# Gate shares by tanh in the graph stage, a root in the last norm, and VectorE sums for the interleaved groups

## What is computed

```python
n   = layernorm(x)                                  # no scale, no offset
agg = epsilon * n + adj @ n                         # per graph, 128x128
h   = silu(rmsnorm(agg @ W1 + b1, rms_weight))      # 512 wide
x   = x + h @ W2 + b2

u   = layernorm(x)
top_v, top_i = top_k(u @ gate_w + gate_b, 2)        # of 16 experts
w   = softmax(top_v)                                # two shares per node
expert(e, u) = relu(u @ w1[e] + b1[e]) @ w2[e] + b2[e]      # 256 wide
moe = w[0] * expert(top_i[0], u) + w[1] * expert(top_i[1], u)
x   = x + layernorm(u + moe) * gamma + beta
```

## Time and profile before

| | |
|---|---|
| median of 3 runs | 896.23 us (894.04 to 896.98) |
| the profiled execution | 895.33 us, span 893.5 us |
| mean granted TensorE clock | 0.955 |
| PE busy | 798.2 us, 89% |
| DVE busy | 644.9 us, 72% |
| ACT busy | 619.6 us, 69% |
| POOL busy | 541.7 us, 61% |
| DMA | 145.20 MB, mean 163 GB/s |

### The profile page before, as it was taken

The page is one execution under the profiler, slowest core; times in us unless marked ns, Lnnn a source line. Parts: engine busy times, 40 slices in busy tenths (PEclk is TensorE's granted clock), DMA queues, the critical chain, the costliest instruction groups (busy, mean ns, idle before and its releaser), DMA issues. The chain is left out here.

```text
span 893.5 us, 20763 instructions
## 1 busy us (share of the span) xinstructions
PE 798.2 (89%) x4835; PEld 593.5 (66%) x4836; DVE 644.9 (72%) x2646; ACT 619.6 (69%) x1327; POOL 541.7 (61%) x572
## 2 busy tenths in 40 slices
PE   5899999999999999943999999999999999999662
PEld 4577777777777777742777777666666666666320
DVE  3688989989999998865566665666766667666444
ACT  2699999999999999841443333666666666666787
POOL 2007766776676767676677777766666656666400
PEclk9799999999999999975999999999999999999875
DMA  5323444333343322217666668877788777777251
GB/s 152 95 72 119 122 121 119 119 119 119 116 119 119 107 83 73 79 54 219 193 200 196 196 210 257 262 223 224 226 241 240 232 232 222 232 223 225 85 193 65
DMA packets 104172, 145.20 MB, mean 163 GB/s; under 512 B 17537, under 2 KB 56855, under 8 KB 104119
## 3 DMA queue, kind: packets, MB, share of 16 engines
q1 hardware_dynamic: 84582, 109.16, 42.8%
q0 software_dynamic: 17344, 34.13, 10.7%
q10 hardware_dynamic: 2192, 1.31, 0.5%
HBM read 99.67 MB, written 46.81 MB: 164 GB/s over the span
## 5 line engine op out<-in xcount | busy, mean ns | idle before, releaser
L467 POOL DMA_INDIRECT combined<-tout,tdest x286 | 282.7, 988 | 131.6 <-issue 73.5
L454 POOL DMA_INDIRECT dispatched<-rows,slot_i x256 | 253.3, 989 | 167.1 <-DVE slot_i L1008 89.8
L782 ACT ACTIVATE hid<-bank,wts 128x256 f32<-128x256 f32 x286 | 119.4, 470 | 169.1 <-PE bank L647 167.5
L662 PE MATMUL bank<-wts,hid 128*128 128x128 f32 x1144 | 165.6, 288 | 0.0
L1117 DVE SCALAR_TENSOR_TENSOR tout<-bank,gate,tin 128x128 f32<-128x128 f32 x286 | 87.1, 346 | 92.5 <-PE bank L662 89.5
L662 PEld LDWEIGHTS bank<-wts,hid 128*128 128x128 f32 x1144 | 138.4, 191 | 17.1
L647 PE MATMUL bank<-tut,wts 128*128 128x256 f32 x572 | 148.6, 383 | 0.0
L502 PEld LDWEIGHTS bank<-w_sb,work 128*128 128x128 f32 x1024 | 122.9, 193 | 17.7 <-issue 14.6
L502 PE MATMUL bank<-w_sb,work 128*128 128x128 f32 x1024 | 126.1, 277 | 1.9 <-ACT work L763 1.9
L496 PE MATMUL bank<-agg,w_sb 128*128 128x512 f32 x256 | 125.0, 611 | 0.0
L647 PEld LDWEIGHTS bank<-tut,wts 128*128 128x128 f32 x572 | 98.6, 193 | 7.6
(11 more groups left out here) (158 smaller groups left out, 1229.1 us busy)
## 6 DMA issues: line engine op xcount, KB each, us to landing
wts<-in_w_exp SPq DMA_DIRECT2D x143, 257.0 KB
tin<-dispatched SPq DMA_DIRECT2D x143, 132.0 KB
moe<-combined SPq DMA_DIRECT2D x32, 512.0 KB
xs<-in_x SPq DMA_DIRECT2D x32, 256.0 KB, 3.0
adj_sb<-in_adj_t SPq DMA_DIRECT2D x32, 256.0 KB
rms_b<-r_row SPq DMA_DIRECT2D x32, 256.0 KB, 3.5
out<-agg SPq DMA_DIRECT2D x32, 256.0 KB, 5.0
combined<-tout,tdest POOLq DMA_INDIRECT x286
```

Of the source, the lines that this page charges most:

```text
L454: nc.gpsimd.indirect_dma_start(dispatched, bass.IndirectOffsetOnAxis(slot_i[:, k, n:n + 1], 0), rows[:, k, n // TOPK, n % TOPK, :], None). ...
L467: nc.gpsimd.indirect_dma_start(combined, bass.IndirectOffsetOnAxis(tdest[:, k, a:a + 1], 0), tout[:, k, a, :], None, bounds_check=TOK * TO ...
L662: last = nc.tensor.matmul(exp_ps[n % 2][:, a * D:(a + 1) * D], hid[:, n % 2, c, a * P:(a + 1) * P], wts[:, k, F + c * D:F + (c + 1) * D], ...
L782: last = nc.scalar.activation(hid[:, n % 2, c, :], hid_ps[n % 2][:, c * TILE:(c + 1) * TILE], ACT.Relu, bias=wts[:, k, F + FC * D + c:F + ...
```

## The change

- DVE writes the difference of the two gate values with its sign to the row (two instructions of 128x4 in place of one of 128x8), and ACT replaces it in the graph stage by tanh(difference / 2), after the first of the four Silus. POOL waits for this (`tanh_done`) in place of `gap_done`. In the tile stage the share is then 0.5 x tanh + 0.5, one DVE instruction; the Exp on ACT and the sum, reciprocal and product on DVE are gone.
- The scale of the last norm is Sqrt on ACT and a reciprocal on DVE, in the next post step, in place of Ln and Exp on ACT.
- For groups 0 to 23 DVE adds the two expert results in SBUF, in place, and takes the statistics there; ACT normalizes from SBUF. PE does no sum for them. The `moe` buffer now holds the sum until ACT has read it, so SP waits for `p_n` in place of `p_y` before it loads a group of the first 24 + 3. Groups 24 to 31 are summed by PE as before.
- One more block of `mixed` is unrolled in front of the loop, which has one turn less.

```diff
+        def summed_by_dve(i, g):
+            return i is not None or g < MIXED
+        def y_of(i, g, k):
+            return moe[:, k, :, 0, :] if summed_by_dve(i, g) else y_ps[k].rearrange("p (j d) -> p j d", d=D)
...
@@ sp, post_step @@
-                    if g >= RING:
-                        sp.wait_ge(p_y, count(i, g - RING + 1))
+                    if i is None and g - RING >= MIXED:
+                        sp.wait_ge(p_y, g - RING - MIXED + 1)
+                    elif g >= RING:
+                        sp.wait_ge(p_n, count(i, g - RING + 1))
...
@@ pool, step @@
-                    pool.wait_ge(gap_done, count(i, g + 1))
+                    pool.wait_ge(tanh_done, count(i, g + 1))
...
@@ pe, post_step @@
-                if has(i, g):
+                if i is None and MIXED <= g < NG:
                     k = g % RING
                     pe.wait_ge(moe_in[k], count(i, g // RING + 1, 16, 1))
-                    if g >= RING:
-                        pe.wait_ge(p_n, count(i, g - RING + 1))
+                    if g - RING >= MIXED:
+                        pe.wait_ge(p_n, g - RING + 1)
...
@@ act, step @@
+                def half_gap(g):
+                    act.wait_ge(gap_done, count(i, g + 1))
+                    gap = rows[:, g % RING, :, :, D + 1:D + 2].rearrange("p j c o -> p (j c o)")
+                    nc.scalar.activation(gap, gap, ACT.Tanh, scale=0.5).then_inc(tanh_done, 1)
+                if not has(i, t) and has(i, t - 3):
+                    half_gap(t - 3)
...
                         nc.scalar.activation(z, z, ACT.Silu, scale=rms_sb[:, c:c + 1]).then_inc(s_done, 1)
+                        if c == 0 and has(i, t - 3):
+                            half_gap(t - 3)
...
@@ act, tile_step @@
-                    if n >= 2:
-                        act.wait_ge(t_gate, count(i, n - 1, 1, RING2 * m))
-                    nc.scalar.activation(share[:, n % 2], tin[:, k, :, D + 1:D + 1 + TOPK], ACT.Exp)\
-                        .then_inc(t_exp, 1)
...
@@ act, post_step @@
-                    nc.scalar.activation(sd[:, 0, k, :], bn[:, 0, k, :, 2], ACT.Ln, bias=ln_eps[:, 0:1],
-                                         scale=1.0 / D).then_inc(p_sd, 1)
-                    act.wait_ge(p_sd, count(i, g + 1))
-                    nc.scalar.activation(rs[:, 0, k, :], sd[:, 0, k, :], ACT.Exp, scale=-0.5).then_inc(p_rs, 1)
+                    nc.scalar.activation(sd[:, 0, k, :], bn[:, 0, k, :, 2], ACT.Sqrt, bias=ln_eps[:, 0:1],
+                                         scale=1.0 / D)\
+                        .then_inc(p_sd, 1)
...
@@ dve, tile_step @@
-                    nc.vector.tensor_tensor(share_sum[:, n % 2], share[:, n % 2, :, 0], share[:, n % 2, :, 1],
-                                            ALU.add).then_inc(t_sum, 1)
-                    dve.wait_ge(t_sum, count(i, n + 1, 1, RING2 * m))
-                    nc.vector.reciprocal(share_inv[:, n % 2], share_sum[:, n % 2]).then_inc(t_inv, 1)
+                    nc.vector.tensor_scalar(gate[:, n % 2], tin[:, k, :, D + 1], 0.5, 0.5, ALU.mult, ALU.add)\
+                        .then_inc(t_gate, 1)
...
@@ dve, post_step, ahead of nb @@
+                    dve.wait_ge(p_sd, count(i, g + 1))
+                    nc.vector.reciprocal(rs[:, 0, k], sd[:, 0, k, :]).then_inc(p_rs, 1)
...
-                    dve.wait_ge(p_y, count(i, g + 1))
+                    if summed_by_dve(i, g):
+                        dve.wait_ge(moe_in[k], count(i, g // RING + 1, 16, 1))
+                        nc.vector.tensor_tensor(moe[:, k, :, 0, :], moe[:, k, :, 0, :], moe[:, k, :, 1, :],
+                                                ALU.add).then_inc(p_sum, 1)
+                        dve.wait_ge(p_sum, count(i, g + 1))
+                    else:
+                        dve.wait_ge(p_y, g - MIXED + 1)
```

More of the change, by code:

```diff
@@ L29 @@
 MIX_FROM = 43
-MIX_TURNS = 5
-MIXED = RING * (3 + MIX_TURNS)
+MIX_TURNS = 4
+MIXED = RING * (4 + MIX_TURNS)
 NQ = NS * E
@@ L151, in gnn_moe @@
         tdest = sb("tdest", [P, RING2, TH], i32)
-        share = sb("share", [P, 2, TH, TOPK])
-        share_sum = sb("share_sum", [P, 2, TH])
-        share_inv = sb("share_inv", [P, 2, TH])
         gate = sb("gate", [P, 2, TH])
@@ L216, in gnn_moe @@
         gap_done = sem("gap_done")
+        tanh_done = sem("tanh_done")
         rank_done = sem("rank_done")
@@ L243, in gnn_moe @@
         t_relu = sem("t_relu")
-        t_exp = sem("t_exp")
-        t_sum = sem("t_sum")
-        t_inv = sem("t_inv")
         t_gate = sem("t_gate")
@@ L253, in gnn_moe @@
         p_y = sem("p_y")
+        p_sum = sem("p_sum")
         p_bn = sem("p_bn")
@@ L294, in tiles_and_groups @@
             span = RING * GB
-            mixed(None, MIX_FROM, -2)
-            mixed(None, MIX_FROM + span, RING - 2)
+            for b in range(3):
+                mixed(None, MIX_FROM + b * span, b * RING - 2)
             with eng.Fori(0, MIX_TURNS) as i:
-                mixed(i, MIX_FROM + 2 * span, 2 * RING - 2)
-            mixed(None, MIX_FROM + (2 + MIX_TURNS) * span, (2 + MIX_TURNS) * RING - 2)
-            for t in range(MIX_FROM + (3 + MIX_TURNS) * span, NT + 1):
+                mixed(i, MIX_FROM + 3 * span, 3 * RING - 2)
+            mixed(None, MIX_FROM + (3 + MIX_TURNS) * span, (3 + MIX_TURNS) * RING - 2)
+            for t in range(MIX_FROM + (4 + MIX_TURNS) * span, NT + 1):
                 tile_step(None, t)
@@ L799, in post_step @@
                     for j in range(GB):
-                        last = nc.scalar.activation(n3[:, k, j, :], y_ps[k][:, j * D:(j + 1) * D], ACT.Identity,
+                        last = nc.scalar.activation(n3[:, k, j, :], y_of(i, g, k)[:, j, :], ACT.Identity,
                                                     bias=nb[:, 0, k, j:j + 1], scale=rs[:, 0, k, j:j + 1])
@@ L956, in step @@
                     last.then_inc(topi_done, 1)
[L957 to L960, removed]
+                    nc.vector.tensor_tensor(rows[:, k, :, 0, D + 1:D + 2], top_v[:, :, 0:1], top_v[:, :, 1:2],
+                                            ALU.subtract)
+                    nc.vector.tensor_tensor(rows[:, k, :, 1, D + 1:D + 2], top_v[:, :, 1:2], top_v[:, :, 0:1],
+                                            ALU.subtract).then_inc(gap_done, 1)
                     dve.wait_ge(topi_done, count(i, g + 1))
@@ L1096, in tile_step @@
                     k = n % RING2
-                    dve.wait_ge(t_exp, count(i, n + 1, 1, RING2 * m))
-                    nc.vector.tensor_tensor(share_sum[:, n % 2], share[:, n % 2, :, 0], share[:, n % 2, :, 1],
-                                            ALU.add).then_inc(t_sum, 1)
-                    dve.wait_ge(t_sum, count(i, n + 1, 1, RING2 * m))
-                    nc.vector.reciprocal(share_inv[:, n % 2], share_sum[:, n % 2]).then_inc(t_inv, 1)
+                    nc.vector.tensor_scalar(gate[:, n % 2], tin[:, k, :, D + 1], 0.5, 0.5, ALU.mult, ALU.add)\
+                        .then_inc(t_gate, 1)
                 b = t - 7
@@ L1106, in tile_step @@
                 if has(i, n, NT):
-                    dve.wait_ge(t_inv, count(i, n + 1, 1, RING2 * m))
-                    nc.vector.tensor_tensor(gate[:, n % 2], share[:, n % 2, :, 0], share_inv[:, n % 2], ALU.mult)\
-                        .then_inc(t_gate, 1)
                     if n >= RING2:
@@ L1125, in post_step @@
                     k = g % RING
+                    dve.wait_ge(p_sd, count(i, g + 1))
+                    nc.vector.reciprocal(rs[:, 0, k], sd[:, 0, k, :]).then_inc(p_rs, 1)
+                g = t - 1
+                if has(i, g):
+                    k = g % RING
                     dve.wait_ge(p_rs, count(i, g + 1))
@@ L1132, in post_step @@
                     k = g % RING
-                    dve.wait_ge(p_y, count(i, g + 1))
+                    if summed_by_dve(i, g):
[5 more added lines that the diff above has]
+                        dve.wait_ge(p_y, g - MIXED + 1)
                     dve.nop(nofuse=True)
                     for q in range(GB // 2):
-                        last = pair_statistics(0, k, q, y_ps[k][:, 2 * q * D:2 * (q + 1) * D]
-                                               .rearrange("p (j d) -> p j d", j=2))
+                        last = pair_statistics(0, k, q, y_of(i, g, k)[:, 2 * q:2 * (q + 1), :])
                     last.then_inc(p_bn, 1)
```

## The result

The changed kernel takes 883.87 us (median of 4 runs, 880.57 to 885.94); the kernel before takes 896.61 us (4 runs, 894.04 to 897.07). The ratio is 0.986, with a 95% interval of 0.982 to 0.990. So it is faster, by 12.7 us (1.4%) and not by 30, and 883.87 lies above the range given. The profiled run took 883.51 us with a span of 881.0 us; its mean granted clock is 0.947 where it was 0.955.

The account below looks back on a forecast made before the run. PE was taken to set the pace before the tail, an ACT-DVE chain in it. 895.3 - 16.5 (tail) - 14 (mixed) + 1 (SP's gate) + 0.5 (graph) + 0.3 (transition) = 866.6, given as 866.5 us; range 855 to 882.

Parts of the forecast that it names:

- What bounds the kernel: Mixed stage: PE sets the pace, 12.43 us a group, with waits of 0.47 for `tut` and 0.42 for `hid`.
- The root: Tail: Sqrt and reciprocal in place of Ln and Exp cut the period from 4.92 to 2.40 us; 16.5 us gained.
- the deduction for the low clock: Tail: PE's two sums at low clock take about 3.8 us a group; gain taken as 16.5 us, not 17.6.
- DVE sums in place of PE: Mixed stage: period falls to 11.8 us, PE standing about 2.2 us for `tut`; 14 us gained, bounds 9 and 20.
- rival 5: Mixed stage: clock falls as PE stands; up to 9.5 us more a group, ten groups give 930 us; 4%.
- SP's gate: Mixed stage: SP waits for `p_n`, so `moe` and later tile loads go later; +1 us, bounds 0 and +27.
- Rival 3: Mixed stage: SP's gate makes tin late in every group, up to 27 us given back, 880 to 893 us; 9%.
- Graph stage, transition, tanh: Graph stage: added Tanh and DVE subtraction lie under existing waits, +0.5 us; transition: two extra DVE instructions, +0.3 us.
- Rival 1: Graph stage: Tanh is not in Silu's table, two loads more a group, 68 us, 935 us in all; 10%.
- Rival 4: Graph stage: no cover for the added instructions, +9 us, 876 us in all; 10%.
- Rival 2: Mixed stage: PE's gain comes through, period 10.3 by POOL, 44 us off in place of 14, 836 us; 4%.
- Direction: Whole kernel: faster 0.85, same 0.02, slower 0.13.

## Why the prediction was right or wrong

- *What bounds the kernel.* Right: PE's order with a wait for `tut` and one for `hid`. A kernel without either has just the forecast's bare tiles and sums (11.25).
- *The root.* Right in kind, short in size in the tail. The tail's period is 2.34 (2.40 forecast) and the stage 18.5 us shorter (16.5 taken); from the second group on each of PE's two sums there took 1.0 to 1.3 us, nearly all at the full-clock figure of 1.02, so the deduction for the low clock was too careful. What I put down to the absence of all table loads, the end of the wait for `hid`, needs only that no second load stand ahead of the Relu (the root alone, still with two loads a group: 11.86).
- *DVE sums in place of PE.* The step itself held: the block is as long as computed (1.11 us where I had 1.07 to 1.28), PE stands for 1.8 to 2.4 us in most groups where it summed (2.2 forecast), and at full clock the mean period is 11.79 (11.8 forecast), down to 11.53 (11.5 named as its lower end). But the gain in that period is the root's, as the 11.84 with PE's sums shows; the sums themselves, moved to DVE, bring next to nothing even at full clock.
- **The step that failed is the sum's treatment of the clock.** The text says that PE stands 2.2 us in every group, and then uses full-clock tiles for all 20 groups, with 4% for rival 5. "In the mixed stage the granted clock was 1.00 with waits of 0.5" was its evidence against the fall, and that is evidence about 0.5, not about the stand of four times that length which my own sum creates. Twelve of 20 groups had the lower level in them, at 13.40 us in place of 11.79: 12 x 1.61 = 19 us, where the forecast had nothing. Without them the stage would have been 20 x (12.44 - 11.79) = 13 us shorter, as forecast; with them it is longer. The idle matmuls bring back 12 to 16 of the 19 us, with a mean period of 11.9 to 12.0. The prediction named this sign of being wrong (a granted clock below 1.00 between 600 and 800 us: it was 0.95 and 0.88). Rival 5 had the event, but with 4% and a price that was too high: up to 9.5 us a group is for a whole group at the lower level, and what was seen is 3.4 us at 0.50, a part of one tile step and of the next, at a cost of about 1.6 us. Its sum has a slip as well: by 9.5 us a group ten groups give 961, not 930.
- *SP's gate.* Right: nothing in the changed kernel (+1 taken). Rival 3's mechanism exists, and shows with DVE's block divided (874.1 against 858.7 with the buffer).
- *Graph stage, transition, tanh.* Right, 0.2 us less than before and not 0.8 more. Rival 1 was wrong as an event, right as a price: the trace of before has the two loads it starts from, 1.28 us ahead of the first Silu (203.12, L763) and 1.28 us ahead of the next Sqrt (206.99, L702), and with Exp in Tanh's place 58 more came. Rival 4 didn't come.
- *Rival 2.* It did not come: it had a period of 10.3, and 11.1 was the shortest that was reached, with two edits more.
- *Direction.* Right, by the root alone. With the parts apart: root -33, tanh 0, DVE sums +18 on top of both (+39 without them).

## What to carry to other kernels

Work taken from the engine that sets the pace brought little here, where it then stood in its place for something else (11.79 us a group at full clock, against 11.84), and a stand longer than any in that stage of the trace has no price there: it is to be measured before the sum relies on it. A change of several parts is worth taking apart, since here one part held the whole gain and another gave more than half of it back. A long block on a helper engine, with a step behind it for which the pacing engine waits, is better divided over several steps: that brought 9 to 11 us with PE's sums in place (865.6 to 854.2; ratios 0.965 and 0.955).

## What the runs showed of the hardware that was not expected

- The granted clock fell to 0.50, for 3.4 us at a time, in a stage in which PE was 83% busy and stood about once in 11.5 us, for 1.8 to 2.4 us; it held with stands of 0.9 to 1.5 us (the kernel with one idle matmul) and of 0.5 us. It doesn't fall in each group: eight of the 20 show nothing of it, and six of these have a stand of 1.8 to 2.1 us too. What decides between them was not found. It fell in the same way behind waits of 1.6 to 1.9 us for a load, and in nearly every group (19 of 20) of the kernel with two stands in each, of 1.6 to 1.8 and about 1.0 us.
- Two idle matmuls in each of 24 groups made the kernel 14 us faster, one made it 16 us faster.
- Silu and Tanh stand side by side with no table load between them, in 29 groups; Silu and Exp don't (a load of 1.28 us on each side of the Exp), and cost (66.3 + 29 x 0.33 of cover) / 58 = 1.31 us a load, an estimate with the cover of rows 2. The load of 1.283 us alone accounts for nearly all of that, and the trace of the changed kernel has 0.6 us of idle before 32 such loads together (L774).
- Where a load of 1.28 us stands in a group counted for more here than how many loads there are: two a group before and two with the root alone, and 0.6 us a group between them (12.44 and 11.86).
